# Edge products of a graph convolution: three tiles of two columns in place of two tiles of three, and a later place for the first product

## The reference

```
def _nnconv(x, src, dst, edge_attr, ew, eb, rw, rb):
    W = (edge_attr @ ew + eb).reshape(E, 16, 16)         # a 16x16 matrix for each edge
    msg = einsum('ei,eio->eo', x[src], W)
    return segment_sum(msg, dst) + x @ rw + rb

h = relu(layernorm(x))
for i in range(3):  h = _nnconv(h, ...);  batchnorm after the first two;  relu
x = x + h @ pred_w + pred_b
h = relu(layernorm(x))
x = x + segment_max(h[src] * edge_weight1, dst) @ W.T + b
```

## Time and profile before

| | |
|---|---|
| median of 3 runs | 10234.24 us |
| the profiled execution's own time | 10232.45 us |
| its span, first to last instruction | 10230.6 us |
| PE busy | 9348.9 us, 91% |
| POOL busy | 7502.7 us, 73% |
| DVE busy | 6967.5 us, 68% |
| ACT busy | 6915.7 us, 68% |
| mean granted TensorE clock | 0.961 of 2.4 GHz |

### The profile page before, as it was taken

How to read it: one execution, slowest core, us unless ns; L and a number is a source line. 1 busy time by engine, 2 the same in 40 slices (tenths; PEclk the granted TensorE clock), 3 DMA queues, 4 the chain that set the end, 5 groups by cost and what they waited for, 6 DMA issues and landing times.

```text
span 10230.6 us, 159899 instructions
## 1 busy us (share of the span) xinstructions
PE 9348.9 (91%) x49036; PEld 8493.2 (83%) x49036; DVE 6967.5 (68%) x10638; ACT 6915.7 (68%) x6857; POOL 7502.7 (73%) x7820
## 2 busy tenths in 40 slices
PE   6999999998599999999849999999993999999994
PEld 4888888887388888888738888888883999999994
DVE  7777777777387878787737787878782544444442
ACT  3777777775377777777627777777763887777772
POOL 6777777777577777777747777777775777777776
PEclk9999999999699999999969999999996999999996
DMA  4333333333233333333323333333331211111121
GB/s 114 94 97 97 97 93 97 97 97 81 59 97 98 93 98 96 97 93 97 89 54 93 97 97 97 93 98 96 98 87 22 45 40 40 40 40 40 40 42 20
DMA packets 373818, 808.28 MB, mean 79 GB/s; under 512 B 151096, under 2 KB 211601, under 8 KB 373528
## 3 DMA queue, kind: packets, MB, share of 16 engines
q0 software_dynamic: 250112, 432.57, 20.5%
q1 hardware_dynamic: 123671, 375.30, 11.6%
HBM read 676.39 MB, written 130.92 MB: 79 GB/s over the span
## 4 chain that ended last, share of the span: by engine, by line
PE 50%; issue 17%; POOL 16%; ACT 13%; DVE 2%; DMA 1%; ACTq 0%; POOLq 0%; DVEq 0%; SPq 0%
PE pY L730 41%; POOL gathered L555 16%; PE pY L752 7%; ACT hot_key L615 6%; ACT apart L610 6%; PE pY L472 2%; DMA gathered<-max_table,idx 1%; ACT xeT L801 1%; PE pT L740 0%; ACTq L242 0%; DVE msg L949 0%; PE pT L461 0%; DVE tmp L278 0%; DVE rank L1060 0%; DVE carry_hi L278 0%
## 5 line engine op out<-in xcount | busy, mean ns | idle before, releaser
L730 PEld LDWEIGHTS pY<-part,hot_key 128*128 128x128 f32 x44640 | 8031.1, 188 | 584.2 <-issue 460.2
L730 PE MATMUL pY<-part,hot_key 128*128 128x400 f32 x44640 | 8446.7, 348 | 55.0 <-DVE xe L867 24.2
L555 POOL DMA_INDIRECT gathered<-conv_table,idx x5580 | 5341.8, 957 | 1885.1 <-issue 1593.4
L867 DVE TENSOR_REDUCE xe<-pY 128x16 f32<-128x400 f32 x5580 | 3127.7, 568 | 1416.2 <-PE pY L730 1407.4
L610 ACT ACTIVATE apart<-key_pair,zone_lane 128x1408 f16<-128x1408 f16 (+1 forms) x1984 | 2859.2, 1488 | 1203.2 <-PE pY L730 974.7
L615 ACT ACTIVATE hot_key<-apart,hot_line 128x1408 fp32r<-128x1408 f16 (+1 forms) x1984 | 3048.4, 1584 | 33.2
L555 POOL DMA_INDIRECT gathered<-max_table,idx x1736 | 1670.3, 962 | 601.4 <-issue 536.9
L949 DVE TENSOR_REDUCE msg<-gathered 128x240 f32<-128x2160 f32 x744 | 1558.6, 2095 | 0.2
L278 DVE TENSOR_TENSOR gathered<-pY,pe_attr 128x432 f32<-128x432 f32 x1488 | 775.8, 563 | 633.1 <-PE pY L752 632.8
L801 ACT COPY xeT<-pT 112x128 f32<-112x128 f32 x744 | 188.8, 254 | 1223.5 <-PE pT L740 1223.5
L752 PE MATMUL pY<-edge_w,xeT 48*128 48x432 f32 (+1 forms) x2976 | 736.5, 544 | 143.1 <-ACT xeT L801 143.1
(11 more groups left out here) (133 smaller groups left out, 1621.8 us busy)
## 6 DMA issues: line engine op xcount, KB each, us to landing
key_pair<-key_rows SPq DMA_DIRECT2D x248, 672.0 KB
scanned<-run_pair SPq DMA_DIRECT2D x248, 416.0 KB, 2.5
gathered<-conv_table,idx POOLq DMA_INDIRECT x5580
attr_pair<-in_attr SPq DMA_DIRECT2D x186, 208.0 KB, 2.5
gathered<-max_table,idx POOLq DMA_INDIRECT x1736
key_pair<-key_rows SPq DMA_DIRECT2D x248, 78.0 KB
conv_table<-gathered SPq DMA_DIRECT2D x36, 360.0 KB, 2.3
conv_table<-rows SPq DMA_DIRECT2D x24, 360.0 KB, 2.3
```

Of the source, the lines that this page charges most:

```text
L555: e.indirect_dma_start(out=G[s][:, t, 0:width], out_offset=None, in_=table[:, :], in_offset=bass.IndirectOffsetOnAxis(ap=idx[s][:, t:t + 1 ...
L730: ins = e.matmul(pG[bank], hot_key[s][:, z, at:at + P], part[:, z * NEAR:(z + 1) * NEAR, :], start=(z == 0 and k == 0), stop=(z == ZONES - ...
L867: e.tensor_reduce(xe[s][:, at:at + D], pG[j % BANKS].rearrange("p (r d) -> p d r", d=D), AX.X, ALU.max).then_inc(s_pick.sem, 1)
```

## The change

A lot becomes three pieces of at most two columns: rows 0 to 31, 32 to 63 and 64 to 95 of `xeT`, by up to 288 columns of `edge_w`. The gaps in `xe` and `edge_w` go. The first two pieces go to the banks that they had, the third to the bank `pT[0]` that holds the transpose (columns 128 to 415 of it). For that, the wait for DVE's multiplication of the product before moves from the product to the turn. A lot has 6 matmul records. Lot 0's product moves behind step 10 of its chunk, and DVE's lot product 0 behind pick 9. The loop for the maximum is left as it is.

```diff
-TRIO = 3
-PIECES = [[(k, min(TRIO, b - a - k)) for k in range(0, b - a, TRIO)] for a, b in LOTS]
-HALF = 64
-DEEP = TRIO * D
-LOT = HALF + DEEP
+PAIR = 2
+PIECES = [[(k, min(PAIR, b - a - k)) for k in range(0, b - a, PAIR)] for a, b in LOTS]
+TILES = 3
+DEEP = PAIR * D
+LOT = TILES * DEEP
...
-        edge_w = sb("edge_w", [LOT, TRIO * ROW])
+        edge_w = sb("edge_w", [LOT, PAIR * ROW])
...
-        pE = pY[0]
+        pE = [pY[0][:, 0, 0:PAIR * ROW], pY[0][:, 1, 0:PAIR * ROW], pT[0][:, P:P + PAIR * ROW]]
...
                 gate(e, "pe", s_pick, number(c) * tp + (b + b_pick))
+
+                gate(e, "pe", s_multiplied, number(c) * 2 + (half + b_mul))
                 e.transpose(pT[0][0:LOT, 0:P], xe[c[1]][:, half * LOT:(half + 1) * LOT], ident[:, :]
...
                 gate(e, "pe", s_xeT, number(c) * 2 + (half + 1 + b_xeT))
-
-                gate(e, "pe", s_multiplied, number(c) * 2 + (half + b_mul))
                 for q, (k, m) in enumerate(PIECES[half]):
-                    rows_of = slice(q * HALF, q * HALF + DEEP)
-                    e.matmul(pE[:, q, 0:m * ROW], xeT[rows_of, :], edge_w[rows_of, 0:m * ROW],
+                    rows_of = slice(q * DEEP, (q + 1) * DEEP)
+                    e.matmul(pE[q][:, 0:m * ROW], xeT[rows_of, :], edge_w[rows_of, 0:m * ROW],
                              start=True, stop=True).then_inc(s_prod.sem, 1)
...
                 pe_turn(e, c1, 0)
-                pe_step(e, c1, HEAD + 5)
+                for j in range(HEAD + 5, HEAD + 7):
+                    pe_step(e, c1, j)
                 pe_product(e, c1, 0)
-                for j in range(HEAD + 6, tp):
+                for j in range(HEAD + 7, tp):
                     pe_step(e, c1, j)
...
-                gate(e, "act", s_prod, number(c) * 4 + (2 * half + b_prod))
+                gate(e, "act", s_prod, number(c) * (2 * TILES) + (TILES * half + b_prod))
...
                 at = j * D
-                if not is_max:
-                    half, k = divmod(j, TH)
-                    at = half * LOT + k // TRIO * HALF + k % TRIO * D
...
-                             pE[:, q, 0:m * ROW].rearrange("p (t d f) -> p t d f", d=D, f=FB),
+                             pE[q][:, 0:m * ROW].rearrange("p (t d f) -> p t d f", d=D, f=FB),
...
-                next_picks(7, 8)
+                next_picks(7, 8, 9)
                 if not is_max and c1 is not None:
                     lot_product(e, c1, 0)
-                next_picks(*range(9, tp))
+                next_picks(*range(10, tp))
...
-        trio = diagonal(TRIO, block[:, :ROW], ROW, bias[:ROW])[:-1]
-        edge_w.append(np.concatenate([trio, np.zeros((HALF - DEEP, TRIO * ROW), np.float32), trio]))
+        edge_w.append(np.tile(diagonal(PAIR, block[:, :ROW], ROW, bias[:ROW])[:-1], (TILES, 1)))
```

More of the change, by code:

```diff
@@ L55 @@
 assert CHUNKS % SLOTS == 0 and CHUNKS <= P and LANES * NB == N and DIGITS == 3 and NEAR <= 2 * ZONES * ZONES
-assert TH <= 2 * TRIO and LOT <= P and TP_MAX * D <= 2 * LOT and TP_CONV >= HEAD + 6 and PE_EDGES <= NB * D
+assert all(len(p) == TILES for p in PIECES) and TH == PAIR * TILES and LOT + PAIR * ROW <= 512 and TP_MAX * D <= 2 * LOT and TP_CONV >= HEAD + 7 and PE_EDGES <= NB * D
 assert W0 * W1 * W2 == EPAD and LOOKS * LOOK == NB and W0 <= P and GB * (W1 + 1) <= 512
@@ L876, in lot_product @@
                     gate(e, "dve", s_pe_factors, number(c) + (b_pefac + 1))
-                gate(e, "dve", s_prod, number(c) * 4 + (2 * half + 2 + b_prod))
+                gate(e, "dve", s_prod, number(c) * (2 * TILES) + (TILES * half + TILES + b_prod))
                 g4 = G[s][:, :, :].rearrange("p t (d f) -> p t d f", f=FB)
@@ L1000, in vec @@
                     pick(e, (0, 0), j)
-                    if j == 8 and not is_max:
+                    if j == 9 and not is_max:
                         lot_product(e, first, 0)
@@ L1022, in edges @@
                     bump(cc, 2 * CHUNKS)
-                bump(s_prod, 4 * CHUNKS)
+                bump(s_prod, 2 * TILES * CHUNKS)
                 bump(s_pe_factors, CHUNKS)
```

## The result

The changed kernel takes 10160.03 us, the median of 4 runs (10157.96 to 10161.15), against 10234.83 us for 4 runs of the kernel before: a ratio of 0.9926, with a 95% interval of 0.9909 to 0.9944. That is 74.8 us less; the profiled execution's own time is 10161.06 us. The forecast was 10160 us.

The account below looks back on a forecast made before the run. PE (18.95 us a chunk) was taken to bound the kernel, POOL's 18.73 close behind; PE falls to 18.09, POOL then gains 74.3 us: 10232.45 - 74.3 = 10158.2, plus 1.8 for the median, 10160 us; range 10150 to 10200.

Parts of the forecast that it names:

- Two limits 0.22 us apart: Conv loops: PE's pace is 18.95 us a chunk, POOL's 18.73; what PE gives back beyond 0.22 is hidden behind POOL.
- PE's pace of 18.09 us: PE's own pace per chunk after the change: 18.95 - 0.38 - 0.48 us.
- the wait: Product 1's wait on PE for its `xeT`, 0.38 us a chunk, goes when product 0 moves one step later.
- a block of 0.68 us: A lot's product block on PE falls from 0.92 to 0.68 us with 288-column tiles; two blocks a chunk give -0.48 us.
- Third tile beside the others: On PE the third tile of a lot runs beside the other two, leaving the block two records deep.
- The rival in which it runs behind them: Third tile runs behind the others on PE: pace 19.45 us a chunk, time 10420 us; tiles-behind outcome given 0.11.
- POOL's gain of 74.3 us: Conv gathers fall to a 944 ns mean, 5341.8 to 5267.5 us busy; it comes off the loops' ends in full.
- What held POOL: POOL takes the wait for the next `idx` several gathers ahead; `idx` late through PE's pace costs a later gather 0.2 us.
- The rival in which POOL stays at 18.95 us: `idx` is late for a reason other than PE, such as blocked DVE writes; nothing gained, 10234 us, chance 0.07.
- The turns' earlier wait: PE's turns now need DVE's lot product earlier; turn 1 has 1.7 us left; cost nothing.
- DVE's third multiplication: A lot has three DVE multiplications instead of two, under 0.1 us more each, hidden in DVE's wait; cost nothing.

Follow-up runs that it names:

- run 1: The kernel before with only product 0 and DVE's lot product 0 moved to their new places, old tiles kept: 10167.31 us, ratio 0.9936.
- run 2: The changed kernel with product 0 and DVE's lot product 0 put back, three tiles of two columns kept: 10160.52 us, ratio 0.9929.
- run 3: The changed kernel with product 0's matmuls issued twice: 10163.67 us, ratio 0.9931 against the kernel before.
- run 4: The changed kernel with both products' matmuls issued twice: 10260.91 us, ratio 1.0027 against the kernel before.
- run 5: The changed kernel with one of each chunk's 15 gathers left out: 9907.41 us, ratio 0.9683 against the kernel before.
- run 6: The kernel before with one of each chunk's 15 gathers left out: 10223.67 us, ratio 0.9992.
- run 8: The changed kernel with the writing of `idx` moved behind pick 4, 0.5 us later: 10157.98 us, ratio 0.9928 against the kernel before.
- run 9: The changed kernel with the writing of `idx` moved behind the scan in the conv loops: 10197.81 us, ratio 0.9966 against the kernel before.
- run 10: The changed kernel with DVE's pick 7 ahead of the scan in the conv loops, `idx` unmoved: 10235.42 us, ratio 1.0002 against the kernel before.
- run 11: The kernel before with the conv loops' scan replaced by a `tensor_reduce` over one element, segmented sum left out: 10224.55 us, ratio 0.9992.

## Why the prediction was right, and where it was not

- **Two limits 0.22 us apart.** Right. Runs 1 to 4 fit only a floor that either part of the change reaches, and runs 5 and 6 show which engine is the floor after and before.
- **PE's pace of 18.09 us.** Right: run 5 lays it bare at 18.09. Its terms were -0.38 for the wait and a block of 0.68 us. In the changed kernel 1.7 us of the wait are left in the whole trace, in run 5, where PE sets the pace, 21 us or 0.06 us a chunk. The block measured 0.69 us.
- **Third tile beside the others.** Right, 0.01 us behind. The rival in which it runs behind them is out.
- **POOL's gain of 74.3 us, off the loops' ends in full.** Right: 74.9 us of gather time, and the three loops are 74.9 us shorter. Part of the exact hit is luck. The profiled execution was forecast at 10158.2 us and took 10161.06, and the median was to stand 1.8 us above it and stands 1.0 us below; the two misses cancel.
- **What held POOL.** Wrong. The step read: "if `idx` is late, a later gather pays about 0.2 us". In the kernel before, `idx` and the scan move together with PE's pace, so one row could not tell them apart. Runs 8 to 11 do: `idx` half a microsecond or 5.5 us later holds nothing of itself, the scan half a microsecond later costs 75 us, and without a scan no gather is long. What happens is this: POOL gains 0.22 us a chunk on DVE until a gather starts inside DVE's scan; from then on each chunk's scan holds that gather by just what POOL would gain. In the kernel before, the hold is an effect of PE's pace, which is why the sum came out all the same. That much is luck too: the sum needed only that the long gathers vanish once POOL sets the pace, and the scan could have kept them.
- **The rival in which POOL stays at 18.95 us.** It did not come, but with 0.07 I priced it by the wrong instruction. Run 10 shows that it was one pick away: in the changed kernel the scan mostly ends between 0.25 us ahead of gather 10's start and 0.2 us behind it, just short of holding it. The slow `idx` writes that this rival rested on are real and cost POOL nothing: in the changed kernel 177 of them start 0.5 to 0.8 us after a gather's start and take 0.30 us in the mean, 189 start at other times and take 0.165 us, and the gathers keep their 944 ns.
- **The turns' earlier wait, DVE's third multiplication.** Right as far as seen: no PE wait on the multiplication shows, and a turn starts 1.57 us after it in the median, where the prediction had 1.7. I didn't test them by themselves.

## What to carry to other kernels

When two engines show the same pace, take the pace of each alone, from a stretch where it is not held or from a run with less work for the other; what a change gives is the distance to the second limit, and parts of a change that each reach it must not be added. A POOL engine that issues DMAs with gaps of 0.3 us can set the time at a busy share of 73%, as here. Once POOL is the bound, look at which DVE instructions run while it issues: their order by itself was worth 75 us here (run 10).

## What the runs showed of the hardware

An indirect DMA's issue on POOL (0.94 us) that starts while a DVE `tensor_tensor_scan` (1.01 us, both inputs in SBUF) runs ends 0.75 us after the scan, 1.75 us after its own start at worst. If the gather started ahead of the scan, it keeps its 0.94 us, and the scan takes at most 0.07 us longer. A `tensor_reduce` over the same tiles holds nothing (run 11, where 124 gathers start inside one and take 0.94 to 0.95 us). That the scan holds POOL is shown by runs 10 and 11; through what it does so is not.

The Trainium skill (SBUF — State Buffer, Who interferes with whom) has DVE and GpSimd share a port pair; where the two contend for it, whoever issues first keeps it for the whole instruction. It has `tensor_reduce` as never contending on trn2. The traces agree for `tensor_reduce`, and for the scan where it comes first. Where the gather comes first they don't: the scan doesn't wait for its end.

Three fp32 matmuls on tiles of 32 rows start within 0.02 us of each other (0.013 us in the median). Each is two records; with 288 columns, the second record of a tile starts 0.35 us behind the first, and each later one 0.24 us behind the one before.
